# Summing 20 instead of 16 low target blocks by gathers in the narrow weighted layers of a graph network

## The reference

```python
x = _layernorm(x + L0(x, edges, edge_attr))     # messages relu(W1 [x[src], attr]) summed by target, then a GRU
x = _layernorm(x + L1(x, edges, W, bias))       # both directions of every edge, counts
x = _layernorm(x + L2(x, edges, W, b, prelu))   # one direction, counts
x = _layernorm(x + L3(x, edges, edge_weight, ...))

def _gcn_conv(x, W, b, src, dst, norm, n_nodes):
    m = x @ W
    msg = m[src] * norm[:, None]
    out = jax.ops.segment_sum(msg, dst, num_segments=n_nodes)
    return out + b
# L3: h = relu(conv(x, W1: 128->256)); h = relu(conv(h, W2: 256->256)); conv(h, W3: 256->128)
```

## Time and profile before

| what | value |
|---|---|
| timed runs | 4233.52 us median of 3 (4227.99 to 4246.55) |
| span of the profiled execution | 4951.5 us |
| instructions | 80811 |
| PE busy | 3982.0 us (80%) |
| DVE busy | 2602.2 us (53%) |
| ACT busy | 1548.4 us (31%) |
| POOL busy | 2555.5 us (52%) |
| mean granted clock of TensorE | 0.869 |

### The profile page before, as it was taken

One profiled execution on the slowest core, in us unless ns is written; L12 is line 12 of the kernel. 1 busy time (PEld: TensorE's weight loads), 2 busy tenths in 40 slices (PEclk: granted clock), 3 DMA queues, 4 the chain that ended last, 5 costly groups with the idle time before them and its releaser, 6 DMA issues. The chain is left out here.

```text
span 4951.5 us, 80811 instructions
## 1 busy us (share of the span) xinstructions
PE 3982.0 (80%) x30230; PEld 2665.0 (54%) x30230; DVE 2602.2 (53%) x5064; ACT 1548.4 (31%) x3170; POOL 2555.5 (52%) x2363
## 2 busy tenths in 40 slices
PE   5787787787788887388887886899888899887888
PEld 5677776677677775244443343444444455443444
DVE  7676555555555556555452334355435556513554
ACT  3334554445455564100000000223134334302332
POOL 4665544554555520266645664566256556505663
PEclk6777878888788888699998998899999999988999
DMA  4445555555566664699976664778655555527776
GB/s 147 125 130 163 190 188 182 189 188 189 186 193 200 196 211 147 188 321 322 303 255 188 204 206 140 272 277 291 223 179 186 175 179 176 190 93 259 261 276 244
DMA packets 612892, 1019.37 MB, mean 206 GB/s; under 512 B 90888, under 2 KB 417575, under 8 KB 612111
## 3 DMA queue, kind: packets, MB, share of 16 engines
q1 hardware_dynamic: 476700, 773.91, 45.6%
q0 software_dynamic: 90848, 199.74, 13.9%
q10 hardware_dynamic: 44956, 40.55, 2.6%
HBM read 737.12 MB, written 276.78 MB: 205 GB/s over the span
## 5 line engine op out<-in xcount | busy, mean ns | idle before, releaser
L951 POOL DMA_INDIRECT x<-p_table,src_i x832 | 953.8, 1146 | 826.0 <-DVE x L711 541.3
L1540 POOL DMA_INDIRECT rows_b<-x_table,low_src x552 | 585.0, 1060 | 540.5 <-POOLq L159 203.6
L930 ACT CAST st_cnt<-ps_mat 128x512 bf16<-128x512 f32 (+1 forms) x825 | 445.7, 585 | 520.8 <-PE ps_deg L845 239.7
L1619 PE MATMUL po_l3b<-mat_l3b,rows_b 128*128 128x512 f32 (+1 forms) x1372 | 580.7, 570 | 32.5 <-DMA mat_l3b<-weights_fwd 25.2
L1540 POOL DMA_INDIRECT rows_a<-h_table,low_src x412 | 441.7, 1072 | 302.1 <-DVE split_l3b L1831 178.2
L860 PE MATMUL ps_mat<-rows_a,hot_s 128*128 128x128 bf16 x4851 | 416.6, 244 | 135.1 <-issue 97.7
L860 PEld LDWEIGHTS ps_mat<-rows_a,hot_s 128*128 128x128 bf16 x4851 | 337.6, 111 | 180.1 <-issue 118.3
L1619 PE MATMUL po_l3a<-mat_l3a,rows_a 128*128 128x512 f32 (+1 forms) x882 | 390.5, 589 | 47.0 <-DMA mat_l3a<-weights_fwd 37.2
L1619 PE MATMUL po_l3c<-mat_l3c,rows_a 128*128 128x512 f32 (+1 forms) x882 | 390.5, 590 | 29.3 <-DMA mat_l3c<-weights_fwd 25.2
L1619 PEld LDWEIGHTS po_l3b<-mat_l3b,rows_b 128*128 128x128 f32 x1372 | 247.6, 200 | 258.5 <-issue 231.4
L1619 PE MATMUL po_l<-mat_l,rows_a 128*128 128x512 bf16 (+1 forms) x1323 | 298.2, 380 | 106.3 <-DVE mat_l L1859 87.1
(11 more groups left out here) (419 smaller groups left out, 7215.9 us busy)
## 6 DMA issues: line engine op xcount, KB each, us to landing
weights_fwd<-st_wt SPq DMA_DIRECT2D x396, 256.0 KB
mat_l<-counts_fwd SPq DMA_DIRECT2D x112, 896.0 KB
mat_l3a<-weights_fwd SPq DMA_DIRECT2D x56, 1792.0 KB
mat_l3c<-weights_fwd SPq DMA_DIRECT2D x56, 1792.0 KB
counts_rev<-st_cnt SPq DMA_DIRECT2D x588, 128.0 KB
rev_l<-counts_rev SPq DMA_DIRECT2D x84, 896.0 KB
mat_l3b<-weights_fwd SPq DMA_DIRECT2D x42, 1792.0 KB
counts_fwd<-st_cnt SPq DMA_DIRECT2D x396, 128.0 KB
```

The lines of the kernel that those rows point to most:

```text
L930: nc.scalar.copy(st_cnt[:, q, :, j * 2 * P:j * 2 * P + n_col], ps_mat[:, f % 3, :].rearrange("p (d c) -> p d c", d=2)[:, :, 0:n_col]).then ...
L951: pool.indirect_dma_start(ring[:, j % RING, t * FD:(t + 1) * FD], None, p_table, bass.IndirectOffsetOnAxis(src_i[:, j * TH + t:j * TH + t ...
L1540: pool.indirect_dma_start(ring[:, j % RL, t, :], None, table, bass.IndirectOffsetOnAxis(low_src[:, j * TH + t:j * TH + t + 1].bitcast(U32), 0)
L1619: mm = nc.tensor.matmul(po[:, p % 2, k, 0:nb * P].rearrange("p (d c) -> p d c", c=P), rows[:, s, k * P:(k + 1) * P], cols, start=(s == 0 a ...
```

## The change

LOWS gets a third entry, 20, and l3a and l3c use it; l1 and l2 keep 16 and l3b 24. In these two layers the dense groups fall from nine to eight, the gathered steps rise from 69 to 86. Since no layer then reads weight matrices of the blocks 16 to 19 (l3b reads from 24 on), the build makes none for them: these four blocks have forward and backward counts only. They get 7 places instead of 13, so the message steps are laid out anew over 517 places instead of 541. A third set of left-over edges is kept, with nine numbers in a record, and the masks of the steps are shared: `low_local` is one tile, and a step's edges of higher blocks are no longer masked but land in columns of `acc` that nobody reads. Three index tiles become bf16.

```diff
-LOWS = (16, 24)
+LOWS = (16, 24, 20)
...
+RECS = 9
...
-        left_rec = nc.dram_tensor("left_rec", [P, T, 8], F32).ap()
+        left_rec = nc.dram_tensor("left_rec", [P, T, RECS], F32).ap()
...
-            dst_blk = sb("dst_blk", [P, T], F32, c)
-            pair2 = sb("pair2", [P, T], F32, c)
-            dst_row = sb("dst_row", [P, T], F32, c)
+            dst_blk = sb("dst_blk", [P, T], BF16, c)
+            pair2 = sb("pair2", [P, T], BF16, c)
+            dst_row = sb("dst_row", [P, T], BF16, c)
...
+                        n = low_steps[1] * TH
+                        chain.step(V.tensor_tensor(in_low[:, 0:n], tmp_f[:, 0:n], same[:, 0:n], ALU.is_le))
+                        chain.step(V.scalar_tensor_tensor(out=low_local[:], in0=in_low[:, 0:n], scalar=FAR,
+                                                          in1=local0[:, 0:n], op0=ALU.mult, op1=ALU.add))
                         for q, up_to in enumerate(LOWS):
...
-                            chain.step(V.tensor_tensor(in_low[:, 0:n], tmp_f[:, 0:n], src_f[:, 0:n], ALU.is_le))
-                            chain.step(V.scalar_tensor_tensor(out=low_local[q][:], in0=in_low[:, 0:n], scalar=FAR,
-                                                              in1=local0[:, 0:n], op0=ALU.mult, op1=ALU.add))
...
-            NARROW = LOWS[0]
+            NARROW, WEIGHED = LOWS[0], LOWS[2]
...
-                return min(u, NARROW) * SUBS + max(u - NARROW, 0) * (NK + SUBS)
+                return min(u, NARROW) * SUBS + max(u - NARROW, 0) * NK + max(u - WEIGHED, 0) * SUBS
...
-                return min(u, NARROW) * 2 + max(u - NARROW, 0) * 8
+                return min(u, WEIGHED) * 2 + max(u - WEIGHED, 0) * 8
...
-                return 1 if n // SUBS < NARROW else 3
+                u = n // SUBS
+                return 1 if u < NARROW else 2 if u < WEIGHED else 3
...
-                return NARROW * (SUBS // 2 + 1) + (u - NARROW) * SUBS + s
+                return WEIGHED * (SUBS // 2 + 1) + (u - WEIGHED) * SUBS + s
...
-                        if u < NARROW:
+                        if u < WEIGHED:
                             return
                         dve.wait_ge(hot_d_ready, m + 1)
                         for v in range(3):
...
+                    chain.step(V.tensor_tensor(far8, open_, kept[2][:], ALU.mult))
...
-                    for q, part in ((5, far5), (6, far6)):
+                    for q, part in ((5, far5), (6, far6), (8, far8)):
...
                         if u < NARROW:
                             mm.then_inc(filled, 1)
+                        if u < WEIGHED:
                             return
...
-                        f = fill_of(u, s, 2)
-                        act.wait_ge(filled, f + 1)
...
+                        if u < NARROW or u >= WEIGHED:
+                            f = fill_of(u, s, 2)
+                            act.wait_ge(filled, f + 1)
...
+                        if u >= WEIGHED:
                             sp.dma_start(weights_fwd[u, :, cols], st_wt[:, q, 0:sub_cols(s)]).then_inc(staged_out[q], 16)
...
-              tables[2], h_table, rows_of(rows_b, HID), rows_of(rows_b, HID), 3, 0, spare_a)
+              tables[2], h_table, rows_of(rows_b, HID), rows_of(rows_b, HID), 3, 2, spare_a)
...
-              m_table, None, None, None, 3, 0, spare_a)
+              m_table, None, None, None, 3, 2, spare_a)
```

More of the change, by code:

```diff
@@ L251, in build @@
             near_low = sb("near_low", [P, T], BF16, c)
-            kept = [sb(f"kept{q}", [P, T], BF16, c) for q in range(2)]
+            kept = [sb(f"kept{q}", [P, T], BF16, c) for q in range(3)]
             deg_left = sb("deg_left", [P, NB, 3], F32, c)
-            total = sb("total", [P, 8], F32, c)
+            total = sb("total", [P, 10], F32, c)
             near_sum = sb("near_sum", [P, 1], F32, c)
@@ L516, in build @@
             x_room = x[:].rearrange("p b f -> p (b f)")
-            rec = rows_a[:, 0:T * 8].rearrange("p (t q) -> p t q", q=8)
-            xt_early = [rows_a[:, 5 * 3 * CB * FD // 2 + h * CB * P:5 * 3 * CB * FD // 2 + (h + 1) * CB * P] for h in range(2)]
+            rec = rows_a[:, 0:T * RECS].rearrange("p (t q) -> p t q", q=RECS)
+            xt_early = [rows_a[:, T * RECS + h * CB * P:T * RECS + (h + 1) * CB * P] for h in range(2)]
             key = sb("key", [P, VT], F32, c)
@@ L568, in build @@
             UN = NB * SUBS
-            NARROW = LOWS[0]
+            NARROW, WEIGHED = LOWS[0], LOWS[2]
             def fills_before(u):
-                return min(u, NARROW) * SUBS + max(u - NARROW, 0) * (NK + SUBS)
+                return min(u, NARROW) * SUBS + max(u - NARROW, 0) * NK + max(u - WEIGHED, 0) * SUBS
             def fill_of(u, s, part):
-                return fills_before(u) + (s if u < NARROW else 3 * s + min(part, len(sub_pairs(s))))
+                if u < NARROW:
+                    return fills_before(u) + s
+                if u < WEIGHED:
+                    return fills_before(u) + 2 * s + min(part, len(sub_pairs(s)) - 1)
+                return fills_before(u) + 3 * s + min(part, len(sub_pairs(s)))
             def fills_of_batch(u, h):
@@ L605, in behind @@
                 for lag in (low, high):
-                    if n - lag in at_place and (lag == low) == (n - lag < place(NARROW - 1, 0)):
+                    if n - lag in at_place and (lag == low) == (n - lag < place(WEIGHED - 1, 0)):
                         return at_place[n - lag]
@@ L754, in _ @@
                     chain.step(V.tensor_tensor(far6, open_, kept[1][:], ALU.mult))
-                    chain.step(V.tensor_reduce(total[:, 0:1], placed[:], AX.X, ALU.add))
-                    chain.step(V.tensor_reduce(total[:, 1:2], far5, AX.X, ALU.add))
-                    chain.step(V.tensor_reduce(total[:, 2:3], far6, AX.X, ALU.add))
-                    V.tensor_scalar(total[:, 1:3], total[:, 1:3], near_sum[:, 0:1], None, ALU.add).then_inc(count_ready, 1)
+                    chain.step(V.tensor_tensor(far8, open_, kept[2][:], ALU.mult))
+                    for q, part in enumerate((placed[:], far5, far6, far8)):
+                        chain.step(V.tensor_reduce(total[:, q:q + 1], part, AX.X, ALU.add))
+                    V.tensor_scalar(total[:, 1:4], total[:, 1:4], near_sum[:, 0:1], None, ALU.add).then_inc(count_ready, 1)
                     dve.wait_ge(filled, fills_before(NB) + 1)
@@ L823, in blocks @@
                         pe.wait_ge(hots_ready, hots_before(u + 1) if h else
[L824 removed]
+                                   hots_before(u) + 1 + (0 if u < WEIGHED else 3))
                         pe.wait_ge(hot_d_ready, m + 1)
@@ L1457, in layer @@
                 mid_ready, planes_ready = sem(f"mid_ready_{name}"), sem(f"planes_ready_{name}")
-                near_at = 4 if both else 5 + lows
+                near_at = 4 if both else (5, 6, 8)[lows]
                 EARLY = 2 if exact else CHKS + 1
```

37 lines of the change are left out of this document (19 added, 18 removed).

## The result

The changed kernel takes 4358.92 us (median of 4, 4357.17 to 4362.68) where the kernel before took 4231.02 us on the same chip (4227.99 to 4246.55): a ratio of 1.0299, interval [1.0275, 1.0323], 3.0% slower. I had forecast 4274 us, range 4160 to 4350. The sign was right, the size was not: +40 us forecast, +128 measured, and the result lies above the range.

A forecast was written before the change was run, and what follows sets the result against it. PE and POOL were taken as nearly balanced, with POOL's gathers in front of l3a and l3c afterwards: build -43, small parts +4, layers +49, carry-over +30 give +40 us, 4274 us; range 4160 to 4350.

The forecast's parts named there:

- The two engines are close to balanced: l3a before the change: PE busy 439.6 of 514 us, POOL occupied 369 us counting 0.30 us behind each gather.
- PE's 29.8 and 49.9 us before L1590: l3a and l3c: PE's idle time ahead of the gathered sums, read as PE already waiting for gathered rows.
- The build: Blocks 16 to 19 without weight matrices: 50 us less on the span (bounds 17 to 75), scaled to -43 us.
- The row: Profile row of L860 in the build: 16.6 us a block, busy plus idle before it, 67 us for four blocks.
- the 16 us of the nine message steps: Build: nine message steps move from blocks 16 to 19 to other blocks, 1.8 us each on PE, taken off the saving.
- Rival 3: Build gains nothing because message gathers pace it, and the layers lose all the same: 4320 us, chance 0.10.
- Small parts: Third set of far edges, larger accumulator clearing, larger record array and VectorE's longer prologue: together +4 us.
- The layers: l3a and l3c with POOL in front, 86 steps for 69: +31 and +22 us, taken as +49 for the pair.
- The carry-over: From span to timed runs: l3a and l3c shrink by 15 us each before the change, +30 us (bounds 0 and +148).
- Rival 2: Faster: POOL not the limit in timed runs, PE stays in front; 4133 us, or near 4178 at 1.15 pitch; chance 0.30.
- Rival 1: No difference: gathers become the bound but cost only what the build gives, POOL's pitch shrinking in timed runs; 4236 us, chance 0.25.
- signs named in advance: Blocks 16 to 19 at 24 to 29 us, build 17 to 75 shorter, little POOL waiting, PE waiting over 90, l3a 515 to 545.

The follow-up runs named there:

- e14: Changed kernel with 69 instead of 86 gathered steps in l3a and l3c, blocks 16 to 19 not summed there; faster kind of chip: 4194.15 us, ratio 0.9901.
- e6: Kernel before with two instead of four gathers in each step of l3a and l3c; slower kind of chip: 4854.12 us, one execution.
- e0: Kernel before, unchanged, profiled again on the faster kind of chip: 4244.18 us with the profile, span 4242.4 us.
- e8: Kernel before with 17 more gathered steps in l3a and l3c, all nine dense groups and all weights kept; slower kind of chip: 5174.53 us, ratio 1.0391.
- e12b: Changed kernel with a ring of six steps instead of four in l3a and l3c; slower kind of chip: 5133.57 us, ratio 1.0298.
- e2: Kernel before with only the build changed: no weight matrices for blocks 16 to 19, l3a and l3c kept at 16 gathered blocks: 4208.41 us, ratio 0.9929.
- e15: Changed kernel with a ring of six steps instead of four in l3a and l3c; faster kind of chip: 4374.68 us, ratio 1.0328.

## Why the prediction went wrong

**What bounds the kernel.** "The two engines are close to balanced" is right for the chip of the timed runs, more so than I could see: e14 and e6 show it from the two sides. The argument for it was wrong, so that it came out right is luck. PE's 29.8 and 49.9 us before L1590 belong to the slower kind of chip; e0 has 2.7 and 3.9. And POOL's 71.5 us of waiting for a converted step, which I took to mean that PE held the ring, were the rows' late arrival: e8 and e12b wait 89.1 and 83.3 us there, with gathers far in front.

**The build, right in size.** -43 us forecast; measured -44.2 in the changed kernel (-44.0 of it in blocks 16 to 19), -37.4 in e2 and -41.0 in e14. By its parts it is less exact. The row gave 16.6 us a block for the 147 matmuls alone, 67 us for four. From that the sum took off the 16 us of the nine message steps that arrive in other blocks, without counting that they leave these four; by its own rows the term was -67, not -50. On the other side the row gave too much for this chip: blocks 16 to 19 were to come from 43.7 to 24 to 29 us each, and they came from 32.2 to 21.2, only 11.0 us a block, with two message steps each gone as well. Of the steps' arrival little is seen: the last 28 blocks, which got most of them, take 895.6 to 900.4 us in the changed kernel, e2 and e14, against 899.4 and 901.4 with the old layout; the first 16 take 288.0 to 293.4 against 285.9 and 287.3 (e15, whose build is longer without a known cause, has 919.4 and 296.4). The granted clock was 0.88 and then 0.80 in the four blocks, where the earlier trace rows had 0.80. These errors, on a stretch measured on another chip, cancel; the near hit is luck. Rival 3, that the build gives nothing, is out.

**Small parts, not seen.** +4 us forecast. The prologue grew by 1.2 us (72.8 to 74.0); the rest is within what unchanged stretches differ by, 7 us.

**The layers, the failed step.** +31 and +22, taken as +49, and 15 for each layer carried over: the two were to cost +79 us. They cost +82.4 and +87.6 = +170. The pitch of the gathers after the change was well forecast: 81 steps at 5.34 us is 432.5 us, and they took from 2554.36 to 2981.89 and one pitch, 428.8. The layer's absolute time was to be 515 to 545 us; it is 527.1. What was wrong is what it is compared with: I set gathers of 1.335 us after the change against a layer before it in which they came every 1.589 us (437.0 us for 276). Held against like, 68 gathers cost 68 x 1.24 to 1.32 = 84 to 90 us, and there is nothing to subtract. The prediction's sentence that the gathers' pitch is nearly constant in its trace (0.95 + 0.30) left out the ring's waits of 71.5 and 76.2 us, which made the pitch 1.589 and not 1.335 there.

**The carry-over.** This is the term of the sum that was mis-sized. I shrank the layer before by a fifth of its profile's excess, 15 us; it shrank by 510.8 - 444.7 = 66 and 513.4 - 434.6 = 79 us. I had put the excess down to the profiler, shrunk the two layers by 30 us together, and bounded this term at 0 and +148; it was +145. The changed layers came out at 527.1 and 522.2 us, 28 us less than the 541.7 and 535.4 that my +31 and +22 gave on the span; in l3a 13 of it is that the ring is let go sooner (2554.36 - 2512.6 = 41.8 us into the layer, not 3120.15 - 3065.5 = 54.7), which is the chip's doing too, since e0 has 38.4. 53 + 145 - 28 = 170, as measured. The bound of +148 stood in the text, and my range had only half of it.

**The rivals.** Rival 2, faster, needed a pitch toward 0.91 us a gather; as a layer's mean it was never below 1.304. Rival 1, gathers in front but at no net cost, asked for a shrinking pitch; it is 0.94 and 0.30 us in the timelines of both kinds. Of the signs named in advance, POOL hardly waiting (10.5 and 11.3 us) held, as did l3a's time and the shorter build; two did not: blocks 16 to 19 at 24 to 29 us each are at 21.2, and PE's wait, which was to be over 90 us, is 82.1 and 89.8, though from 2.7 and not from 30. The Trainium skill, DMA: Bandwidth & Descriptors, section Anatomy of one DMA, calls descriptor generation small. Here 68 more gathers cost 84.0 and 90.1 us with the ring nearly never in the way (e15), so the trace doesn't agree that issuing them is cheap, though it doesn't part descriptor generation from the rest of POOL's 0.94 and 0.30 us.

## What to carry to other kernels

Where two engines are balanced, moving work from one to the other costs its full price on the side that gets it and earns next to nothing on the side that gives (here 84 and 90 us against 7 and 2): count each engine's time with the gap behind every instruction, not its busy share, and look at both engines' waits for each other, since the chain of waits may name only one, as e0's did. If span and timed median differ by far more than the timed runs do among themselves, settle why before any term of the sum is taken from the profile: here the narrow layers had another limit on another chip. And a bound that you can't argue away belongs in the range.

## What the runs showed of the hardware

**Gathers come at two rates.** In l3a and l3c, with all four gathers of a step, a gather of 128 rows starts every 1.30 to 1.36 us on the faster kind of chip and every 1.56 to 1.61 on the slower, with rings of four or six steps and with or without the dense group. POOL's instruction is the same on both (1034 and 1035 ns, e0 and the earlier trace rows), so the difference lies behind the issue. Why, no run shows. The changed kernel as it is was not run on the slower kind; with a ring of six it was (e12b).

**A TensorE that waits runs at a lower granted clock.** In l3a, e14 and the changed kernel multiply the same 784 dense matmuls. Where PE waits 32.0 us for gathered rows (e14) the granted clock is 0.96 and the mean matmul 575 ns; where it waits 82.1 us (changed) they are 0.90 and 607 ns, and the group takes 362.5 us instead of 337.0. With e0's 2.7 us they are 0.97 and 573 ns, with e12b's 132.8 us 0.85 and 624 ns. So more of the stretch ran at 1.2 GHz instead of 2.4, behind an engine that had stood idle longer. This and 204 more gathered matmuls are why PE's busy time stayed at 419 us though 98 dense matmuls of 42 us went. In the layer's time no cost of it is seen, since PE was waiting anyway and what lies outside the gathers stays at 70 us.

**VectorE beside gathers.** POOL's and VectorE's timeline of the changed kernel in the build:

```profile
702.28 2.43 POOL L961 DMA_INDIRECT x<-p_table,src_i  x1 [0.30 <-issue]
...
706.27 0.94 POOL L961 DMA_INDIRECT x<-p_table,src_i  x1 [0.30 <-issue]
707.51 1.75 POOL L961 DMA_INDIRECT x<-p_table,src_i  x1 [0.30 <-issue]
```

```profile
701.87 2.02 DVE L695 TENSOR_TENSOR hot_s<-iota,slots 128x3584 bf16<-128x3584 bf16 x1 [2.66 <-PE ps_mat L869]
...
706.36 2.09 DVE L706 TENSOR_TENSOR rows_a<-rows_a,slots 128x1792 bf16<-128x1792 bf16 x2
```

All 525 gathers of this trace with no VectorE instruction beside them last 938 to 955 ns. The one that began at 706.27, just ahead of a product of two SBUF tensors, is such a short one; the next, inside the product, took 1.75 us. The 100 message gathers that began inside one of L706's products last 1.50 us at the median, the 99 that began inside one of L695's 2.16; that of 702.28, with three VectorE operations beside it one after the other, took 2.43. Not every VectorE operation does it: the 68 that began inside L718's sum of a PSUM and an SBUF tensor last 0.94 at the median. It is an observation; no run took the products away. Something of the kind may be why the layers' mean pitch, not the shortest, was the right end; that is not shown.
